# A decoder layer on one core: the first slot steps and the passage from slot attention to cross attention in another order

## The reference

```
x = x + slot_attention(layernorm(x))          # 4 heads, 64 slots, gates, a scan over positions
x = x + cross_attention(layernorm(x), ctx)    # 16 heads of 8, two biases and a mask before the softmax
x = x + experts(layernorm(x))                 # 8 experts with low-rank parts, each position weighted by its top 2
```

## Time and profile before

| | |
|---|---|
| runs | 603.99, 604.25, 606.11 us, median 604.25 |
| profiled execution | 605.81 us, of which 604.1 us span |
| busy | TensorE 90%, VectorE 80%, ScalarE 66%, GpSimd 59% of the span |
| TensorE clock granted | 0.962 of full, as a mean |

### The profile page before, as it was taken

The page is one execution under the profiler, slowest core; times in us unless marked ns, Lnnn a source line. Parts: engine busy times, 40 slices in busy tenths (PEclk is TensorE's granted clock), DMA queues, the critical chain, the costliest instruction groups (busy, mean ns, idle before and its releaser), DMA issues.

```text
span 604.1 us, 17291 instructions
## 1 busy us (share of the span) xinstructions
PE 542.7 (90%) x5328; PEld 416.1 (69%) x5328; DVE 482.7 (80%) x1945; ACT 398.6 (66%) x1033; POOL 355.7 (59%) x362
## 2 busy tenths in 40 slices
PE   4689999999998559999999999999978999999986
PEld 3457777777776436777777777777766778788864
DVE  2478887887886358999999999999988688888872
ACT  2668878878775238889999999999965333333221
POOL 6234555456544657888888888888933233334430
PEclk9799999999998868999999999999987899999999
DMA  6910000000000075898989888888700000000000
GB/s 169 239 21 2 1 1 1 0 0 0 2 0 2 7 126 101 153 168 152 159 155 156 155 155 149 148 151 162 128 3 1 2 17 19 17 17 19 17 19 17
DMA packets 84429, 42.47 MB, mean 70 GB/s; under 512 B 4378, under 2 KB 84132, under 8 KB 84388
## 3 DMA queue, kind: packets, MB, share of 16 engines
q1 hardware_dynamic: 83234, 41.63, 37.5%
q10 hardware_dynamic: 1154, 0.33, 0.2%
HBM read 39.86 MB, written 2.10 MB: 69 GB/s over the span
## 4 chain that ended last, share of the span: by engine, by line
PE 50%; DVE 17%; issue 16%; ACT 7%; POOL 7%; DVEq 0%; ACTq 0%; POOLq 0%
PE banks L873 6%; PE banks L907 6%; PE banks L920 5%; PE banks L453 5%; ACT c_P L954 4%; PE banks L1228 4%; DVE c_P L1026 3%; DVE shared L714 3%; PE banks L1252 3%; PE banks L896 3%; PE banks L417 2%; PE banks L444 2%; PE banks L499 2%; PE banks L886 2%; DVE banks L687 2%
## 5 line engine op out<-in xcount | busy, mean ns | idle before, releaser
L1121 POOL TENSOR_TENSOR c_bias<-c_fside,c_cm 128x2048 f32<-128x2048 f32 x32 | 146.2, 4568 | 27.5 <-PE banks L873 16.9
L954 ACT ACTIVATE c_P<-c_P,c_min 128x128 f32<-128x128 f32 x512 | 156.7, 391 | 2.9 <-DVE c_min L1026 2.9
L1026 DVE CUSTOM_DVE_ANT_0 c_P<-banks,c_bias 128x128 f32<-128x128 f32 x512 | 116.4, 284 | 5.6 <-issue 3.0
L907 PEld LDWEIGHTS banks<-ident,c_P 128*128 128x128 f32 x512 | 59.3, 144 | 30.0 <-issue 23.2
L907 PE MATMUL banks<-ident,c_P 128*128 128x128 f32 x512 | 76.0, 282 | 3.7 <-DVE shared L1062 3.7
L1062 DVE COPY shared<-banks 128x512 f32<-128x512 f32 x96 | 65.7, 685 | 0.0
L1228 PE MATMUL banks<-um,lb_s 128*128 128x512 f32 x192 | 56.1, 407 | 2.7 <-ACT shared L1285 1.9
L1464 POOL TENSOR_TENSOR xs<-shared,xs 128x512 fp32r<-128x512 f32 x8 | 10.7, 1337 | 69.9 <-ACT xs L1295 69.9
L1285 ACT ACTIVATE shared<-banks,bi_col 128x512 f32<-128x512 f32 x32 | 22.0, 687 | 39.2 <-PE banks L1228 39.2
L1228 PEld LDWEIGHTS banks<-um,lb_s 128*128 128x128 f32 x192 | 34.6, 190 | 19.1 <-ACT shared L1285 12.5
L794 POOL TENSOR_TENSOR shared<-shared 128x512 f32<-128x512 f32 x16 | 20.4, 1275 | 38.1 <-ACT shared L585 38.1
(11 more groups left out here) (195 smaller groups left out, 1310.6 us busy)
## 6 DMA issues: line engine op xcount, KB each, us to landing
c_fside<-in_fside_Bx16xSxS_dram SPq DMA_DIRECT2D x64, 512.0 KB, 7.2
c_ctx<-in_ctx_dram SPq DMA_DIRECT2D x32, 64.0 KB, 5.2
out_dram<-shared SPq DMA_DIRECT2D x8, 256.0 KB, 2.3
X<-in_x_dram SPq DMA_DIRECT2D x3, 512.0 KB, 5.4
kmask_sb<-in_mask_BxS_bf_dram SPq DMA_DIRECT2D x1, 512.0 KB, 6.8
X<-in_x_dram SPq DMA_DIRECT2D x2, 128.0 KB, 3.0
c_P<-in_L_ffn_wi_dram SPq DMA_DIRECT2D x1, 256.0 KB
c_P<-in_L_ffn_lora_B_dram SPq DMA_DIRECT2D x1, 256.0 KB
```

The source lines that it names most:

```text
L907: last = nc.tensor.transpose(bank(2 + i % 2)[:, 128 * j:128 * j + 128], P[:, q, XG * i + j, :], ident[:])
L954: last = nc.scalar.activation(P[:, par, h, :], P[:, par, h, :], ACT.Exp, bias=mn[:, par, h:h + 1], scale=-1.0)
L1026: last = nc.vector.tensor_tensor_reduce(out=P[:, o, h, :], in0=bank(SCORE_BANKS[i])[:, 128 * j:128 * j + 128], in1=fm[:, o, h, :], scale=- ...
L1121: nc.gpsimd.tensor_tensor(fm[:, q, :, :], fs[:, q, :, :], bc(cm[:], XH), ALU.add).then_inc(C["fm"], 1)
```

## The change

Every tick and step function takes a further argument `only`, a set of piece names; a piece is written when its stage exists and its name is in the set (or no set is given). The order inside one call stays that of the function: the order of the names in a call says nothing. `parts` of the cross steps goes away and is replaced by names with the same order at the far end of the cross attention.

1. First slot steps. ScalarE: in ticks 0 and 1 the gate functions come before `gsa_normalise` of the next pair. TensorE: tick 1 turns the inputs before the decay sums; tick 2 has attention, turned inputs, decay sums, queries/keys/gates, and only then the slot logits. VectorE: the sigmoid product (silu) is first in ticks 1 and 2.
2. Passage. The pieces of ticks 16 to 19 and steps -3 to 3 take turns one by one on four engines, as written below. GpSimd makes the bias sum of sequence 0 directly after tick 16.
3. Banks. The scores of sequences 0, 1 and 2 use banks 1, 4, 5 and again 1; the fourth product waits until VectorE has read the first.
4. `masks` on VectorE moves from the start of step n (sequence n+2) to the end of step n (sequence n+3), which is the same place in a run of whole steps.
5. The cross loop starts at m=2 in place of 1 and runs as many times; two steps more are written out before it and two fewer after it.

```diff
+def named(only):
+    return lambda flag, name: flag and (only is None or name in only)
...
+        FIRST_BANKS = (1, 4, 5, 1)
+        FIRST = 3
+        def score_banks(batch):
+            return FIRST_BANKS if isinstance(batch, int) and batch < FIRST else SCORE_BANKS
...
+                places = score_banks(n + 1)
                 for i in range(NI):
                     rows = slice(32 * i, 32 * i + 32)
-                    nc.tensor.matmul(bank(SCORE_BANKS[i]), qx[rows, o, :], kbd[rows, o, :, :].rearrange("p j s -> p (j s)"),
+                    if places[i] in places[:i]:
+                        need(pe, C["tt"], 4 * n + 5 + places.index(places[i]))
+                    nc.tensor.matmul(bank(places[i]), qx[rows, o, :], kbd[rows, o, :, :].rearrange("p j s -> p (j s)"),
...
         # GpSimd's program
             pool.wait_ge(G["xn"], PAIRS)
             x_peeled(cross, -3)
-            gsa_peeled(gsa, PAIRS + 1)
+            gsa_peeled(gsa, PAIRS)
...
             x_peeled(cross, -2)
+            gsa_peeled(gsa, PAIRS + 1, "outputs")
+            x_peeled(cross, -1)
+            gsa_peeled(gsa, PAIRS + 1, "squares")
+            gsa_peeled(gsa, PAIRS + 1, "weights")
+            x_peeled(cross, 0)
             gsa_peeled(gsa, PAIRS + 2)
-            x_peeled(cross, -1)
+            x_peeled(cross, 1)
             gsa_peeled(gsa, PAIRS + 3)
...
         # ScalarE's program
-            for t in range(0, 2):
-                gsa_peeled(gsa, t)
+            gsa_peeled(gsa, 0, "inputs", "gates")
+            gsa_normalise(act, 1)
+            gsa_peeled(gsa, 1, "inputs", "sigmoids", "decays", "gates")
+            gsa_normalise(act, 2)
+            gsa_peeled(gsa, 1, "slots")
...
-            x_peeled(cross, -3)
-            gsa_peeled(gsa, PAIRS + 1)
+            gsa_peeled(gsa, PAIRS + 1, "turned", "roots")
             x_peeled(cross, -2)
-            gsa_peeled(gsa, PAIRS + 2)
+            gsa_peeled(gsa, PAIRS + 1, "exps", "outputs")
             x_peeled(cross, -1)
+            x_peeled(cross, 0, "exps1", "exps2", "inputs", "exps3")
+            gsa_peeled(gsa, PAIRS + 2, "turned")
+            x_peeled(cross, 0, "exps0", "keys", "queries", "turned3")
+            gsa_peeled(gsa, PAIRS + 2, "roots")
+            x_peeled(cross, 1, "exps1")
+            gsa_peeled(gsa, PAIRS + 2, "outputs")
+            x_peeled(cross, 1, "exps2", "inputs", "exps3", "exps0", "sums", "keys", "queries", "turned3")
             gsa_peeled(gsa, PAIRS + 3)
...
         # VectorE's program
-            gsa(1, 1, False, True, False, False, False, True)
+            gsa(1, 1, False, True, False, False, False, False, ("silu",))
+            gsa(1, 1, False, True, False, False, False, True, ("statistics", "slots", "values"))
...
-            gsa_peeled(gsa, 2)
+            gsa_peeled(gsa, 2, "silu")
+            gsa_peeled(gsa, 2, "statistics", "attention", "logits", "slots", "sums", "values", "gates")
...
-            x_peeled(cross, -3)
-            gsa_peeled(gsa, PAIRS + 1)
+            x_peeled(cross, -3, "statistics", "aggregates")
+            gsa_peeled(gsa, PAIRS)
             dve.wait_ge(s_km, 16)
-            x_peeled(cross, -2)
-            gsa_peeled(gsa, PAIRS + 2)
-            x_peeled(cross, -1)
+            x_peeled(cross, -3, "normalise", "masks")
+            gsa_peeled(gsa, PAIRS + 1, "attention")
+            x_peeled(cross, -2, "statistics", "aggregates")
+            gsa_peeled(gsa, PAIRS + 1, "logits")
+            x_peeled(cross, -2, "normalise", "masks")
+            gsa_peeled(gsa, PAIRS + 1, "mix", "sums")
+            x_peeled(cross, -1, "scores0", "scores1", "scores2", "scores3")
+            gsa_peeled(gsa, PAIRS + 1, "stream")
+            x_peeled(cross, -1, "statistics", "aggregates", "values", "normalise", "masks")
+            x_peeled(cross, 0)
+            gsa_peeled(gsa, PAIRS + 2, "mix")
+            x_peeled(cross, 1, "statistics", "scores0")
+            gsa_peeled(gsa, PAIRS + 2, "stream")
+            x_peeled(cross, 1, "turned0", "scores1", "turned1", "scores2", "aggregates", "scores3", "outputs", "turned2", "stream",
+                     "values", "normalise", "masks")
+            x_peeled(cross, 2)
             gsa_peeled(gsa, PAIRS + 3)
...
         # TensorE's program
-            gsa_peeled(gsa, 1)
+            gsa_peeled(gsa, 1, "inputs")
+            gsa_peeled(gsa, 1, "decays", "gates", "values", "slots")
...
-            gsa_peeled(gsa, 2)
+            gsa_peeled(gsa, 2, "inputs", "attention")
+            gsa_peeled(gsa, 2, "decays", "gates")
+            gsa_peeled(gsa, 2, "logits", "values", "slots")
...
-            x_peeled(cross, -3)
-            gsa_peeled(gsa, PAIRS + 1)
+            gsa_peeled(gsa, PAIRS + 1, "attention", "turned", "squares")
             pe.wait_ge(G["silu"], PAIRS)
             x_peeled(cross, -2)
-            gsa_peeled(gsa, PAIRS + 2)
-            pe.wait_ge(G["lgts"], PAIRS)
+            gsa_peeled(gsa, PAIRS + 1, "logits", "mix")
+            pe.wait_ge(G["shift"], PAIRS)
+            x_peeled(cross, -1, "scores")
+            gsa_peeled(gsa, PAIRS + 1, "outputs", "project")
+            x_peeled(cross, -1, "inputs", "queries", "values")
+            x_peeled(cross, 0, "scores")
...
+            x_peeled(cross, 0, "turned0", "inputs")
+            pe.wait_ge(G["x1"], PAIRS - 2)
+            x_peeled(cross, 0, "turned1", "queries")
+            gsa_peeled(gsa, PAIRS + 2, "turned")
+            x_peeled(cross, 0, "turned2", "turned3", "values")
+            pe.wait_ge(C["ptD"], 3)
+            gsa_peeled(gsa, PAIRS + 2, "squares", "mix")
+            x_peeled(cross, 1, "scores")
+            pe.wait_ge(C["ptA"], 1)
+            gsa_peeled(gsa, PAIRS + 2, "outputs", "project")
...
+            x_peeled(cross, 1, "turned0", "inputs")
+            pe.wait_ge(G["x1"], PAIRS - 1)
+            x_peeled(cross, 1, "turned1", "mix", "queries", "turned2", "turned3", "values", "outputs")
+            pe.wait_ge(C["ptD"], 6)
+            gsa_peeled(gsa, PAIRS + 3, "squares")
             pe.wait_ge(G["un"], PAIRS)
-            x_peeled(cross, -1)
-            gsa_peeled(gsa, PAIRS + 3)
+            x_peeled(cross, 2, "scores")
...
+            x_peeled(cross, 2, "turned0", "inputs", "turned1", "mix", "queries", "turned2", "turned3", "values", "outputs")
+            pe.wait_ge(C["ptA"], 3)
+            gsa_peeled(gsa, PAIRS + 3, "project")
+            x_peeled(cross, 3, "scores", "turned0", "inputs")
```

More of the change, by code:

```diff
@@ L500, in project_out @@
                 last.then_inc(G["y"], 1)
-            if intra:
+            on = named(only)
+            if on(intra, "attention"):
                 attention()
-            if mix:
+            if on(mix, "turned"):
                 weights_turned()
-            if finish:
+            if on(finish, "squares"):
                 square_sums()
-            if turn:
+            if on(turn, "decays"):
                 decay_sums()
-            if intra:
+            if on(intra, "logits"):
                 slot_logits()
-            if gate:
+            if on(gate, "inputs"):
                 x_turned()
-            if mix:
+            if on(mix, "mix"):
                 slot_mix()
-            if gate:
+            if on(gate, "gates"):
                 queries_keys_gates()
-            if turn:
+            if on(turn, "values"):
                 values()
-            if mix:
+            if on(mix, "outputs"):
                 outputs()
-            if turn:
+            if on(turn, "slots"):
                 s_turned()
-            if finish:
+            if on(finish, "project"):
                 project_out()
@@ L609, in roots @@
                 nc.scalar.activation(rr[:], rt[:], ACT.Exp, scale=-0.5).then_inc(G["r"], 1)
-            if turn:
+            on = named(only)
+            if on(turn, "decays"):
                 decays()
-            if mix:
+            if on(mix, "turned"):
                 weights_turned()
-            if finish:
+            if on(finish, "roots"):
                 root_logs()
-            if turn:
+            if on(turn, "sigmoids"):
                 sigmoids()
-            if finish:
+            if on(finish, "roots"):
                 roots()
-            if gate:
+            if on(gate, "inputs"):
                 x_turned()
-            if turn:
+            if on(turn, "decays"):
                 decay_exps()
-            if ahead:
+            if on(ahead, "normalise"):
                 gsa_normalise(act, t + 1)
-            if intra:
+            if on(intra, "exps"):
                 slot_exps()
-            if gate:
+            if on(gate, "gates"):
                 absolutes()
+            if on(gate, "gates"):
                 exps()
+            if on(gate, "gates"):
                 logs()
-            if mix:
+            if on(mix, "outputs"):
                 outputs()
-            if turn:
+            if on(turn, "slots"):
                 s_turned()
@@ L730, in statistics @@
```

(31 more changed lines are left out.)

231 lines of the change are left out of this document (116 added, 115 removed).

## The result

The changed kernel takes 674.58 us (median of 4 runs, 668.06 to 677.71), beside 605.18 for the kernel before on the same chip (4 runs, 603.99 to 608.08): ratio 1.1125, 95% interval 1.1032 to 1.1218. Forecast were 598 and a range of 592 to 602.5, with 0.05 for slower. The profiled execution is the slowest of the four: 677.71 us, span 676.0. Ratios leave out executions in a slower state; among the runs of the kernel before beside e5 to e11 there are two of 17, 994.43 and 996.64 us, which nothing here explains.

What follows compares the result with a forecast made beforehand. The prediction took the passage to be bound by a loop of waits through engine queues, not work. Median 604.25 less 5.5 (passage) and 1.0 (start) gave 597.75, said as 598; its own range 595 to 601, overall 592 to 602.5.

Steps and rivals of the forecast that it cites:

- C: Passage rival: slower, TensorE stays at 1.2 GHz from first fourth product to scores of sequence 3; 607.8 us, chance 0.06.
- Steps 1 to 3: Start: gate functions first, pair 1's gates at full clock, VectorE's setup pieces equally earlier; 5.1 us gained so far.
- step 2: Start: TensorE idles about 1.4 us, clock holds, pair 1's gates end at 20.8; at 1.2 GHz about 23.0.
- Steps 4 and 5: Start, ticks 2 and 3: logits behind gates leave 3.0 us gained; falling clock around attention costs about 2.0; net +1.0.
- Passage, steps 1 to 3: Mask 0.55 us later; first bias sum at 195.1, not 205.08; first three scores 202.35, not 215.49; then 2.6 us idle.
- Passage, steps 3 to 6: Fourth-product waits, low clock and late GpSimd work shrink the lead: sequences 1, 2, 3 earlier by 13.9, 10.1, 6.5 us.
- Step 5: Passage: TensorE busy from 214.3, full clock back near 218.5; scores of sequence 2 at 223.3, 10.1 us earlier.
- step 3: Passage: first three score products at 202.35, not 215.49; the fourth waits for VectorE, leaving TensorE idle 2.6 us.
- D: Rival: the edits do little, since the slot chain alone may set the passage; 604 us, chance 0.05.
- B: Rival: fourth-product waits and late GpSimd squares eat the gain; passage +2, start 0; 602.3 us, chance 0.18.
- Both signs of being wrong: Steady cross steps (7.1 us) or experts changing at all; scores of sequence 3 coming less than 4 us earlier.

Runs made afterwards that it cites:

- e5: Kernel after with 40 VectorE padding instructions and the first three ticks in the order of before; 605.39 us, ratio 1.0018.
- e11: Kernel after with 128 padding instructions spread over VectorE's early waits, its cross loop at 695; 679.88 us.
- e2: Kernel before with only the cross loop starting at m=2 (two more steps before, two fewer after), VectorE's loop at 566; 656.38 us, ratio 1.0841.
- e1: Kernel after with 40 padding instructions at the head of VectorE's program, its cross loop at 607 instead of 567; 605.77 us, ratio 0.9998.
- e3: Kernel after with 16 padding instructions on VectorE, its cross loop at 583; 605.15 us.
- e12: Kernel after with a cross loop body of half the length (two steps per pass) on every engine, VectorE's again from 567; 606.23 us, ratio 1.0014.
- e7: Kernel after with 40 VectorE padding instructions and the fourth score product of sequences 0, 1 and 2 issued behind other work; 599.9 us, ratio 0.9907.
- e6: Kernel after with 40 VectorE padding instructions and tick 2 alone back in its old order (gates after logits); 600.32 us, ratio 0.9939.
- e10: Kernel before with 112 padding instructions spread over VectorE's early waits, its cross loop at 562; 658.81 us.
- e4: Kernel after with 8 padding instructions on VectorE, its cross loop at 575; 669.08 us.

## Why the prediction was wrong

**The step that failed** is in its first part: "The end of the cross attention, the loop bodies and the experts keep their order (masks at the end of step n stands next to the start of step n+1), so I put them at nothing; a difference of a few tenths of us from other instruction addresses would be all." Its second place is the last sentence of the passage: "Code cost of the further written-out steps: nothing at the best row, below 0.5 us." Neither was worked out from a row. The addresses were what the change moved most: VectorE's body went from 450, where it lies over three blocks, to 567, where it lies over four. e2 shows the edit alone at +8.4%, e1, e3 and e12 show the kernel after without the stalls at the time of before. The cost: 59.9 of the 72.5 us between the spans of the kernel after and of e1 (676.0 and 603.5) are the ten stalls; I put the other 12.6 down to the clock behind them: after each of the five jumps TensorE has 1.2 GHz for 13.7 to 17.1 us, the first time from 292.0 to 305.7. No run took this apart. None of the rivals had it; C, the slower one, names another mechanism.

**Start.** Steps 1 to 3 ran in e1 as told: ScalarE's gate function at 12.54 (forecast 12.4), gates of pair 1 at full clock (19.16 to 21.1, forecast 18.7 to 20.8). In the profiled executions of the kernel after and of e7 they ran at 1.2 GHz (granted clock 0.50 from 19.0 to 22.4 in the kernel after), the other bound of step 2. TensorE of the kernel after in order of time:

```profile
16.47 0.41 PE L403 MATMUL banks<-ident,shared 128*128 128x128 f32 x2 [1.35 <-ACT shared L537]
...
18.97 2.04 PE L411 MATMUL banks<-shared,g_wqkf 128*128 128x256 f32 x4 [0.98 <-DVE shared L672]
20.81 1.81 PE L413 MATMUL banks<-g_wqkf,shared 128*128 128x256 f32 x4
```

In e1 the same products took 1.10 and 1.03. It too has an idle stretch of 1.35 us, only one group of products earlier (before 15.57), and 0.43 us ahead of the turned inputs. So with the same order the step can fall either way, and the length of one idle stretch, by which I took 1.4 us as safe, does not decide it. Steps 4 and 5 were right and dear. Logits of pair 0 end at 31.6 in e1 (forecast 31.4), attention takes 2.08 us, and of the 1.0 us forecast for the start e1 has 0.4 at the logits of tick 16 (184.49, before 184.87). The sum held. That its step 4 gives back 2.1 of the 5.1 us won before it and step 5 another 2.0 was in its own terms; leaving tick 2 alone brings them back, as e6 shows.

**Passage, steps 1 to 3.** Right, in the kernel after: first bias sum at 194.96 (forecast near 194), scores of sequence 0 at 201.61 (near 201), the fourth 3.6 us later, with 2.45 us of idle time before it and low clock after.

**Passage, steps 3 to 6, the size.** Forecast distances of sequences 1 to 2 and 2 to 3 were 11.6 and 10.8 us; e1 has 14.2 and 12.2. Sequence 3 comes 1.4 us earlier than before (0.7 at sequence 4), not 6.5. In times of the trace before, 5.5 us are missing at sequence 3 (6.5 forecast, 1.4 less the start's 0.4 measured). Two terms were mis-sized.

```profile
201.43 1.13 PE L894 MATMUL banks<-shared,c_q 32*128 32x512 f32 x6 [1.15 <-DVE shared L705]
...
212.76 2.08 PE L894 MATMUL banks<-shared,c_q 32*128 32x512 f32 x6
...
226.95 1.13 PE L894 MATMUL banks<-shared,c_q 32*128 32x512 f32 x6
...
239.17 1.14 PE L894 MATMUL banks<-shared,c_q 32*128 32x512 f32 x8
```

The first is the lone fourth product, for which the sum has no length of its own; a quarter of the four would be 0.5, 0.5 and 0.3 us. It measured 2.07, 2.07 and 1.13 in e1: at either clock as long as the other three together (two matmuls 2.07 us beside six 2.08; 1.13 beside 1.13) and as all four in one go (1.14). The four have 32 rows each and run side by side, so one taken out of them saves nothing and adds a full one: 1.6 + 1.6 + 0.8 = 4.0 us, an estimate from these rows.

The second is the clock. Step 5 has it back near 218.5, 16.2 us after the first scores. In e1 it came back at 223.5, 22.1 us after them, with TensorE busy all of the time from 218.5 on, and fell once more from 230.4 to 233.8. In the profiled execution of e6, with the same passage and the same lone products, it came back after 19.9 us and did not fall again, and from sequence 0 to 3 it took 36.0 us (198.50 to 234.52) where e1 took 37.7: 1.7 us are the clock's alone. The idle stretches before the fourth products came out shorter than the 2.6 us of step 3 (2.23, 1.63 and 1.29 in e1), and the terms overlap, so how the 5.5 us divide is not shown to the tenth. What e7 shows is that the wait, with the low clock behind it, is the part that can be hidden: 4.0 us came back at sequence 3 though the product is as long as ever.

The Trainium skill, page "TensorE: Matmul & The Clock Gate", section "Part 3: Packing small matmuls — row/col tiling", has this: tiles on different row groups run at the same time, and the span of several is little more than that of one. The rows agree (two matmuls 2.07 us, six 2.08), and the earlier trace rows alone could have told it: four products of 32 rows in 1.14 us.

**The rivals, against the 605.8 us of e1**, which is what the order of the change does without the stalls. By number D (the edits do little; 604) is nearest, but its reason is wrong, since sequence 0 came 14 us earlier. By mechanism it is B (the new wait eats the gain; 602.3) with a part of C (607.8): TensorE had 1.2 GHz for 24 of the 38 us from the first scores to those of sequence 3. Both signs of being wrong that the prediction gave came true: the cross steps lost time at each jump, and sequence 3 came only 1.0 us earlier (1.4 in e1).

**Open.** Why a stall at the jump is 5 to 8 us long for a packet of 0.7 us. Why the second stall is at most 1.9 us with the old body (e2, e10) and 3.2 to 5.6 with the new one (after, e11): the instructions around the edge differ, and no run tried that alone. Whether 576, 577 or 578 is the edge.

## What to carry to other kernels

When a change writes steps out before a loop or after it, count VectorE's instructions up to the loop and in its body: the loop's place is part of the change, and a stall "<- issue" at each jump together with more packets on an instruction queue is its sign. By arithmetic a loop body of up to 257 instructions lies over at most three blocks of 128 wherever it starts; of such bodies only the one of 142 was run, and it cost 0.34 us per jump. A product taken out of a group that runs side by side costs a whole one, and a wait added in TensorE's queue wants other work issued ahead of it.

## What was not expected of the hardware

- VectorE's instructions come in blocks of 128 (packets of 8192 bytes). A body of 282 stays over three blocks (a jump costs 0.2 to 0.3 us) and is fetched again over four: 4.6 to 7.9 us at the jump and, with the body of the kernel after, 3.2 to 5.6 at the next edge, or one stall of 8.0 to 13.9 us (e4).
- Padding alone moved the same work by 54 us (604.62 to 658.81); 12 instructions more, nothing else.
- Only VectorE's loop showed this. ScalarE's body was 134 instructions and GpSimd's 44, too short to lie over four blocks. TensorE's was longer than VectorE's: 298 instructions as written, and in 28.4 us of e1, about one pass, the trace has 398 products and 399 weight loads. It showed no such stall in any run, and q8, the other queue that brings instructions, has 20 or 21 packets on every page, of 16384 bytes each. So the rule of three blocks of 128 is measured for VectorE alone.
